# Chunk 3's decays repeated by DMA, convolution of z on VectorE, heads 0 and 1 made once, shares repeated in pieces

## The reference

```
x = norm(x + mamba_mixer_and_mlp(x))     # stage 0
x = norm(x + latent_attention_and_moe(x))# stage 1: 16 heads of 8, 7 routed experts, top 2
x = norm(x + linear_attention(x))        # stage 2: 4 heads of 64
x = norm(x + binary_mlp(x))              # stage 3
x = norm(x + attention(x))               # stage 4: 16 heads, score width 128
x = norm(x + moe(x))                     # stage 5: 8 experts of 256, top 2, gelu
x = norm(x + pruned_attention(x))        # stage 6: 16 heads of 64, keys masked by head 0's scores
x = norm(x + moe(x))                     # stage 7: 8 experts of 176, top 2, plus shared ones
```

```
xs, zs = split(in_proj(ln(x)));  xc, zc = silu(conv4(xs) + bx), silu(conv4(zs) + bz)
delta  = softplus(dt(xc));  dA = exp(delta * A);  dBu = delta * B * u
h_t    = dA_t * h_{t-1} + dBu_t;  y_t = sum over states of h_t * C_t
out    = out_proj(concat(y + u * D, zc))
S  = relu(masked scores of head 0);  FF = cumulative sum of shifted S;  att = att - FF
keep the 51 keys with the smallest FF and the diagonal, per query, for all heads
```

## Time and profile before

| | before |
|---|---|
| median of the runs | 1339.64 us |
| the profiled execution: time, span | 1339.95 us, 1338.2 us |
| TensorE busy | 1285.8 us, 96% |
| TensorE weight loads | 910.6 us, 68% |
| VectorE busy | 922.5 us, 69% |
| ScalarE busy | 909.0 us, 68% |
| GpSimd busy | 768.9 us, 57% |
| mean granted TensorE clock | 0.978 |
| moved by DMA | 67.87 MB |
| chain that ended last | 82% TensorE, 6% ScalarE, 5% GpSimd, 5% VectorE |

### The profile page before, as it was taken

The page is one execution under the profiler, slowest core; times in us unless marked ns, Lnnn a source line. Parts: engine busy times, 40 slices in busy tenths (PEclk is TensorE's granted clock), DMA queues, the critical chain, the costliest instruction groups (busy, mean ns, idle before and its releaser), DMA issues.

```text
span 1338.2 us, 26178 instructions
## 1 busy us (share of the span) xinstructions
PE 1285.8 (96%) x8764; PEld 910.6 (68%) x8764; DVE 922.5 (69%) x3611; ACT 909.0 (68%) x2503; POOL 768.9 (57%) x845
## 2 busy tenths in 40 slices
PE   8999789999998999999999999999999999999997
PEld 4445356567754777678777777777788877876665
DVE  5777998868757677757566454797597678764244
ACT  6667899777585789675868565557577758755221
POOL 2878877568539477476665755447534525442525
PEclk9679999999998999999999999999999999999999
DMA  8744000110042000102000101201200021004230
GB/s 291 190 127 108 1 2 1 57 57 2 1 142 85 1 2 2 57 24 104 4 1 1 64 1 38 92 1 64 83 2 1 2 80 17 2 1 135 55 103 24
DMA packets 23109, 67.87 MB, mean 51 GB/s; under 512 B 2336, under 2 KB 9120, under 8 KB 20672
## 3 DMA queue, kind: packets, MB, share of 16 engines
q1 hardware_dynamic: 22976, 66.20, 15.6%
HBM read 62.85 MB, written 3.34 MB: 49 GB/s over the span
## 4 chain that ended last, share of the span: by engine, by line
PE 82%; ACT 6%; POOL 5%; DVE 5%; issue 1%; DMA 1%; SPq 0%; POOLq 0%; DVEq 0%; ACTq 0%
PE bank L1193 71%; PE bank L1197 11%; ACT arena L1651 3%; POOL arena L2461 1%; ACT L1651 1%; POOL arena L2465 1%; DVE arena L1912 1%; ACT bank L1651 1%; DVE stats L1926 1%; DVE stats L1915 1%; POOL arena L2524 1%; POOL stats L2452 0%; DVE arena L2091 0%; POOL arena L2474 0%; DVE stats L1929 0%
## 5 line engine op out<-in xcount | busy, mean ns | idle before, releaser
L1651 ACT ACTIVATE arena<-arena 128x256 f32<-128x256 f32 (+4 forms) x804 | 355.8, 446 | 50.1 <-POOL arena L2517 26.5
L1651 ACT ACTIVATE arena<-bank 128x512 f32<-128x512 f32 (+2 forms) x347 | 183.8, 560 | 204.4 <-PE bank L1193 135.1
L1193 PE MATMUL bank<-XT,W 128*128 128x512 f32 (+1 forms) x752 | 293.3, 525 | 0.0
L2474 POOL TENSOR_TENSOR arena<-arena 128x512 f32<-128x512 f32 (+1 forms) x108 | 170.6, 1595 | 153.4 <-DVE arena L1912 50.0
L1193 PEld LDWEIGHTS bank<-W,arena 128*128 128x128 f32 x1888 | 227.9, 192 | 39.2 <-issue 32.0
L1193 PE MATMUL bank<-W,arena 128*128 128x128 f32 x1888 | 238.2, 276 | 1.3 <-DVE arena L2173 0.8
L1193 PE MATMUL bank<-arena 128*32 128x256 f32 (+8 forms) x2912 | 225.5, 334 | 9.8 <-POOL arena L2484 2.7
L2523 POOL TENSOR_TENSOR arena<-arena 128x256 f32<-128x256 f32 x192 | 119.2, 621 | 189.2 <-DVE arena L2163 188.9
L1193 PEld LDWEIGHTS bank<-arena 128*32 128x32 f32 (+4 forms) x2912 | 152.8, 152 | 83.4 <-issue 48.2
L2524 POOL TENSOR_TENSOR arena<-arena 128x512 f32<-128x512 f32 x192 | 201.5, 1049 | 0.0
L1197 PE MATMUL bank<-CF,arena 128*128 128x128 f32 x1312 | 184.0, 277 | 12.0 <-POOL arena L2524 5.3
(11 more groups left out here) (143 smaller groups left out, 1670.2 us busy)
## 6 DMA issues: line engine op xcount, KB each, us to landing
arena<-rws SPq DMA_DIRECT2D x8, 2048.0 KB, 7.5
arena<-rep SPq DMA_DIRECT2D x62, 256.0 KB, 5.3
arena<-rws SPq DMA_DIRECT2D x4, 1792.0 KB, 6.4
W<-w SPq DMA_DIRECT2D x2, 2124.0 KB, 8.2
arena<-rws SPq DMA_DIRECT2D x8, 384.0 KB, 10.1
W<-w SPq DMA_DIRECT2D x1, 2692.0 KB, 9.5
XT<-wkq SPq DMA_DIRECT2D x4, 512.0 KB, 6.0
W<-w SPq DMA_DIRECT2D x1, 2005.0 KB, 15.7
```

The source lines that it names most:

```text
L1193: return e.matmul(o, lhsT, rhs, start=start, stop=stop, skip_group_check=True)
L1651: return e.activation(o, a, func, **kw)
L2474: e.tensor_tensor(h, h, w, ALU.mult).then_inc(has["gw"], 1)
```

## The change

**Decays of chunk 3.** `BY_DMA = (3,)`. For this chunk `0.da` goes. `0.wd` writes delta to DRAM (`repd`), 16 `0.rd` read it repeated into two tiles in SBUF in turn, `0.dd` takes the exponential there, and the scan reads decay and h from SBUF.

```diff
+                elif name == "0.wd":
+                    on.wait_ge(*emptied(u("b", "0.dt", c)))
+                    e.dma_start(repd[c], step0(c, 0)).then_inc(d_wd[c], 16)
+                elif name == "0.rd":
+                    g = group0(n)
+                    on.wait_ge(d_wd[c], 16)
+                    if n >= 2:
+                        on.wait_ge(*scanned(c, n - 2))
+                    e.dma_start(spread0(c, n), repd[c][8 * g:8 * g + 8, :].unsqueeze(0).to_broadcast([16, 8, 512])).then_inc(d_rd[c][n % 2], 16)
...
+                elif name == "0.dd":
+                    g, a = group0(n), spread0(c, n)
+                    on.wait_ge(a_mat, 4)
+                    on.wait_ge(d_rd[c][n % 2], 16 * (n // 2 + 1))
+                    act(later(a), later(a), ACT.Exp, scale=am[:, g:g + 1], bias=am[:, 16 + g:17 + g]).then_inc(has["dA"], 1)
...
+                    if c in BY_DMA:
+                        on.wait_ge(*after("dA", "0.dd", c, n))
+                        e.tensor_tensor_scan(h, spread0(c, n), h, 0.0, ALU.mult, ALU.add).then_inc(has["st"], 1)
...
+        def spread0(c, q):
+            return ar(c, 9784 + q % 2 * 512, 512)
+
+        def scanned(c, q):
+            return after("st", "0.st", c, q) if c in BY_DMA else emptied(decays0(c, q))
```

```diff
+                    if n:
+                        mm(ps[:, :], wt(0, "win")[:, 128:256], s0(c, 1)).then_inc(full[b.i], 1)
+                        continue
...
+                    own(ts(s0(c, 7), bank[b.i][:, :], wt(0, "tz")[:, 1:2], None, ALU.mult))
+                    for k in (0, 2, 3):
+                        lo, hi = max(0, 1 - k), 256 - max(0, k - 1)
+                        on.wait_ge(*own.last())
+                        ins = stt(o3[:, :, lo:hi], z3[:, :, lo + k - 1:hi + k - 1], wt(0, "tz")[:, k:k + 1], o3[:, :, lo:hi], ALU.mult, ALU.add)
```

```diff
+        def heads6(c, u, n, i):
+
+            return head0(c, n, 1) if (u, i) == (4, 0) else (k6 if n else q6)(c, u)[:, i * 256:(i + 1) * 256]
+
+        def fresh6(u):
+
+            return (1,) if u % 4 == 0 else (0, 1)
...
-                        for i in range(2):
+                        for i in fresh6(n):
                             ins = mm(ps[:, i * 256:(i + 1) * 256], wt(6, w)[:, (2 * m + i) * 128:(2 * m + i + 1) * 128], xt)
```

```diff
+        for k in range(5 if s == 7 else 4):
+            add("er", k, ("ew", 0))
...
+                    if n < 4:
+                        E = slice(2 * n, min(2 * n + 2, BLOCKS[s] - SHARED[s]))
+                        m = (E.stop - E.start) * 512
+                        e.dma_start(to[:, 1024 * n:1024 * n + m], w[E, :].rearrange("e t -> (e t)").unsqueeze(0).to_broadcast([128, m])
+                                    ).then_inc(d_er[c][n], 16)
```

More of the change, by code:

```diff
@@ L271, in stage_steps @@
             add("0.h", j, ("0.m", 0))
-        add("0.o", 0, *[("0.h", j) for j in range(4)])
+        add("0.x", 0, ("0.y", 0), ("0.b", 0, PREP))
+        add("0.o", 0, ("0.x", 0), *[("0.h", j) for j in range(4)])
         add("0.e", 0, ("0.o", 0))
@@ L311, in stage_steps @@
         add("4.vz")
-        add("4.v", 0, ("4.vz", 0))
-        add("4.r", 0, ("load", 0, PREP, 4))
+        add("4.v", 0, ("4.vz", 0), ("4.c", 0, PREP))
         for i in range(16):
             add("4.qk", i, ("load", 0, PREP, 4), *([("4.ex", last_reader(i - 5))] if i >= 5 else []))
-        attention(lambda u: [("4.r", 0)] + [("4.qk", u // 2 * 4 + k) for k in range(4)], lambda u: [("4.v", 0)])
+        attention(lambda u: [("4.v", 0)] + [("4.qk", u // 2 * 4 + k) for k in range(4)], lambda u: [("4.v", 0)])
         add("4.y", 0, *[("4.pv", u) for u in range(UNITS)])
@@ L711, in order_of_steps @@
             if tiled(x) != tiles:
-                more = 0.16 if t < free[g] + 0.1 else 0.09
+                more = (0.0 if tiles == "q" else 0.095) if t < free[g] + 0.1 else 0.09
             elif t > free[g] + 0.1:
@@ L786, with network @@
 ROOM = 10912
[L789 removed]
+def network(nc, x, ws, wkq, cf, cb, rep, repd, rws, gs, out):
     with ExitStack() as ctx:
@@ L1311, in _ @@
                     w2 = wt(0, "w2") if s == 0 else bw3[:, 512:1024]
-                    if s == 0:
-                        for j in range(4):
-                            mm(ps[:, j * 128:(j + 1) * 128], cst("one", 1), wt(0, "b2", 0, 1), j == 0, False)
                     for j in range(4):
@@ L1436, in _ @@
                     on.wait_ge(*after("rt_w", "1.rt" if s == 1 else f"{s}.r", c))
-                    w = s3(c, 0) if s == 5 else router(s, c)
-                    for j in range(4 if s == 5 else 1):
-                        ins = e.transpose(bank[b.i][:, j * 128:(j + 1) * 128], w[:, 32 * j:32 * j + 128], cst("ident"))
-                    ins.then_inc(full[b.i], 1)
+                    e.transpose(bank[b.i][:, 0:128], router(s, c), cst("ident")).then_inc(full[b.i], 1)
                 elif name in ("1.up", "7.up"):
@@ L1535, in _ @@
                 elif name == "4.v":
-                    b, ps = first(name, c)
-                    for j in range(4):
-                        ins = mm(ps[:, j * 128:(j + 1) * 128], cols_(4, c)[:, j * 128:(j + 1) * 128], wt(4, "wv"))
-                    ins.then_inc(full[b.i], 1)
-                elif name == "3.b":
+                    on.wait_ge(*after("rk", "4.c", PREP))
+                    for k, (b, ps) in enumerate((first(name, c), second(name, c))):
+                        for j in range(2):
+                            js = slice((2 * k + j) * 128, (2 * k + j + 1) * 128)
+                            ins = mm(ps[:, j * 144:(j + 1) * 144], cols_(4, c)[:, js], values4())
+                        ins.then_inc(full[b.i], 1)
+                elif name in ("0.b", "3.b"):
                     b, ps = first(name, c)
@@ L1564, in _ @@
                     ins.then_inc(full[b.i], 1)
-                elif name == "4.r":
-                    b, ps = first(name, c)
-                    for k in range(4):
-                        on.wait_ge(*emptied(u("b", "4.a", PREP, k)))
-                    for j in range(4):
-                        ins = mm(ps[:, j * 16:(j + 1) * 16], cols_(4, c)[:, j * 128:(j + 1) * 128], pre[:, 48:64])
-                    ins.then_inc(full[b.i], 1)
                 elif name == "4.qk":
@@ L1726, in _ @@
                     b = u("b", name, c, n)
-                    on.wait_ge(*filled(b))
-                    act(s0(c, 6 + n), bank[b.i][:, :], ACT.Silu, bias=wt(0, "czb" if n else "cxb")).then_inc(done[b.i], 1)
+                    if n:
+                        on.wait_ge(*emptied(b))
+                        act(s0(c, 7), s0(c, 7), ACT.Silu, bias=wt(0, "czb")).then_inc(has["zc"], 1)
+                    else:
+                        on.wait_ge(*filled(b))
+                        act(s0(c, 6), bank[b.i][:, :], ACT.Silu, bias=wt(0, "cxb")).then_inc(done[b.i], 1)
                 elif name == "0.bc":
```

228 lines of the change are left out of this document (133 added, 95 removed), and 537 rows, old and new, of tables (EMITS, OPENS, PARTS, TURNS).

## The result

The changed kernel took 1357.63 us (median of 4 runs, 1354.12 to 1361.34) against 1339.80 for the kernel before, beside it on the same chip: ratio 1.0121, 95% interval 1.0095 to 1.0148, slower by 13 to 20 us. The forecast was 1331, its range 1310 to 1348, with 0.60 on faster. Over all sets of runs the kernel before lay between 1337.0 and 1347.8 us. The execution profiled after took 1354.93 us, span 1352.8.

What follows compares the result with a forecast made beforehand. TensorE was taken as the bound where saturated, with four engines near a common limit from 100 to 200 us. Terms -15.5 - 4 + 11 = -8.5 us gave 1331 us, own range 1322 to 1336, full range 1310 to 1348.

Steps and rivals of the forecast that it cites:

- TensorE's work removed, without the bias of `0.o`: Heads 0 and 1 once 6.9 us, 4.r in 4.v 2.9, 5.wt transposes 1.3, 5.bb 0.4, all counted as gain.
- bias of `0.o` off TensorE, `0.x` on GpSimd: Four one-row matmuls per chunk go for one 0.b: 4.0 us gained; 0.x's 1.3 us per chunk covered by 0.m and 0.h.
- convolution of z on VectorE: TensorE loses 7.7 us over chunks 2, 0 and 1, VectorE gets 2.8 a chunk: -4 us, from -8 to +6.
- chunk 3 by DMA: Chunk 3's scan stretch 14.1 us longer, 3.1 filled by 4.qk steps and 4.b: +11 us net, from +5 to +20.
- Work taken off TensorE is worth its full length wherever the stretch is saturated.: Rule for pricing removed TensorE work: full length in saturated stretches, only a part in the first 250 us.
- all of the 15.5 us: Matmul time removed from TensorE, placed after 230 us at 93 to 100% busy and all counted; bounds 12 and 16.
- half of what TensorE loses: Convolution of z: -4 us, with VectorE's work free for chunk 2 and up to 5.7 us on the path for chunks 0 and 1.
- two buffers and a round of repeat, exponential and scan: Chunk 3: each two states need one round, landing 4.0 us plus exponential, scan and semaphores: 6.2 us (5.3 to 7.5).
- that was so before: Chunk 3's exponentials need ScalarE's table, which 1.up of chunk 1 changes; taken as unchanged from before, no cost given.
- rival 2: Chunk 3's DMA round trip between 0.rd and 0.st makes the kernel slower: landing 5.3 us, round 7.5, 1351 us; chance 0.23.
- 0.1 us: Chunk 3: each scan longer by this with both operands in SBUF, 1 us in seven rounds, left in the range.
- the 12 at which I had said that I would be wrong: Sign against the prediction: a gain under 12 us outside the stretch of chunk 3's scans.

Runs made afterwards that it cites:

- e10: Kernel before, old order, with heads 0 and 1 once, 4.r in 4.v, one 5.wt transpose, masks, er pieces; chunk 3, z, 0.o bias stay on TensorE: 1335.6 us.
- e7: All edits of the changed kernel, chunk 3 by DMA and z on VectorE included, in the step order of the kernel before: 1371.1 us, ratio 1.0233 to before.
- e11: e10 plus only the bias of 0.o made as in the change (0.b once, 0.x on GpSimd): 1344.6 us, ratio 1.0023 to before.
- e12: e10 plus only the convolution of z on VectorE, for all four chunks: 1345.1 us, ratio 1.0022 to before.
- e5: Changed kernel's edits in the old order, but chunk 3's steps repeated by TensorE and not by DMA; z on VectorE: 1355.0 us, ratio 1.0104 to before.
- e1: Changed kernel in its new order, with chunk 3's steps repeated by TensorE into PSUM again: 1353.3 us, ratio 1.0081 to before.
- e2: e1 with the convolution of z back on TensorE too, for all four chunks: 1356.3 us, ratio 1.0116 to before.
- e14: Changed kernel in its new order, with the bias of 0.o by four one-row matmuls again, no 0.x: 1359.3 us, ratio 1.0143 to before.
- e15: Edits of e10 in the changed kernel's new order (chunk 3, z and bias of 0.o by TensorE): 1355.1 us, ratio 1.0103 to before.
- e4: e3 with each chunk 3 repeat waiting for the exponential two states back instead of its scan: 1346.6 us, ratio 1.0051 to before.
- e9: Kernel before, leaving out the matmuls for heads 0 and 1 in 6.qk of units 0 and 4 (values wrong): 1338.2 us, ratio 0.9962.
- e13: e11 with 0.x moved in GpSimd's order to right before the eviction of 0.o: 1338.6 us, ratio 0.9971 to before.
- e3: Changed kernel, with ScalarE writing chunk 3's exponentials into PSUM so its scans have one PSUM operand: 1353.9 us, ratio 1.0090 to before.
- e8: Changed kernel, with GpSimd's multiplications beside chunk 3's scans cut to 8 of 512 columns (results left out): 1355.8 us, ratio 1.0100 to before.

## Why the prediction was wrong

**The sum, term by term.** Starting from e10, edits on the old order add up: 1335.6 + 9.0 (`0.x`) + 9.6 (z) + 16.1 (chunk 3) = 1370.3, and e7, which has them all, took 1371.1. The changed kernel, with the order written for them, took 1357.6.

| term | forecast | measured, old order |
|---|---|---|
| TensorE's work removed, without the bias of `0.o` | -11.5 | -5.4 (-7.5 to -3.1), e10 |
| bias of `0.o` off TensorE, `0.x` on GpSimd | -4.0 | +9.0, e11 |
| convolution of z on VectorE | -4 | +9.6, e12 |
| chunk 3 by DMA | +11 | +16.1, e7 - e5 |
| the order of all steps rewritten | no term | -13.5, changed - e7 |
| sum | -8.5 | +15.8 (by the ratio 1.0121: +16.2) |

The last row but one is what is left over, so the sum is bound to come out; only e7 above is a check on it. Undone one by one in the new order, the same edits are worth much less: chunk 3 by DMA +4.3 us (changed - e1), z -3.0 (e1 - e2), `0.x` -1.6 (changed - e14), none of them clear of noise. With all three undone (e15) the kernel is still 13.8 us above the one before by its ratio. So in the changed kernel itself no single edit holds the loss. It goes with the new order (and the bank numbers that follow from it), in which e1 to e4 are slow too.

**1. "Work taken off TensorE is worth its full length wherever the stretch is saturated."** This is the step that failed first. The earlier trace rows gave 100.00 busy of 100.00 us, and I took all. e10, which has this term alone, got 5.4 us (3.1 to 7.5) of 11.5; e9 got about 0.7 of its 6.9. Time in which TensorE is busy can cover a wait for another engine: where a 6.qk step's removed matmuls had stood over such a wait, it showed as 0.60 us of idle time for GpSimd, and `4.r` at 427.66 had stood over 1.8 us of one. Not all that is missing has been found this way. I had also put all of the 15.5 us after 230 us. Three of the four bias steps of `0.o` in it lie at 112, 127 and 206 us, where TensorE was 84 to 93% busy, so by my own rule only a part of their 3 us should have counted.

**2. `0.x` costed at nothing.** I named its cover (`0.m` and `0.h`) and asked who waits for it. I didn't ask what it waits for and what is queued behind it on GpSimd. In the old order that is 9.0 us, 6.0 of them by its place (e13). In the changed kernel's own order it costs nothing that could be measured (e14), but the 4.0 us forecast as its gain didn't come either.

**3. z: "half of what TensorE loses".** VectorE at 89% was in the earlier trace rows and I had +6 as the end of the range; the old order gives +9.6. I had them free for chunk 2 and in part on the path for chunks 0 and 1; e12 shows 0.9 us for chunk 2 and 3.0 between two scans for chunk 0. In the new order no difference could be measured (e1 against e2). The profile of the changed kernel was 6 us ahead of before from 240 to 335 us, about as forecast, and lost that again by 400.

**4. Chunk 3.** The stretch was forecast at 46.7 us and measured 53.6 by the same two marks (398.33 to 451.94). The mechanism, two buffers and a round of repeat, exponential and scan, is right (e4: early repeats take 6.6 us off). The sizes: landing 3.4 us and not 4.0, which should have made it shorter; scans 1.92 and not 1.21, 11 us in all, of which 5 to 7 reach the path (e3, e8; with short scans e8's stretch is 46.9 us by the same marks); one round of 10.6 us by the order on ScalarE and VectorE, of which the prediction said "that was so before". It wasn't: before, no round took over 5.3 us. Pairs came 7.0 us apart ((447.24 - 398.33) / 7), where 6.2 was forecast and 7.5 stood for rival 2. Rival 2 had the right place and sign, with 1351, and wrong reasons (landings of 5.3 us).

I had weighed the scan's new form by two adds, 0.800 and 0.685 us, and put "0.1 us" into the range. Those two rows don't bear on it: nothing says what GpSimd did beside them. The Trainium skill has the rule in full (SBUF — State Buffer, Who interferes with whom): a VectorE instruction with two SBUF inputs contends with a GpSimd instruction that reads SBUF, the ports that they share are an exclusive lock, and issue order decides which of them waits. By that rule a scan waits for the rest of a 1.26 or 2.34 us instruction, and the trace agrees: scans of 1.2 us with none beside them or one that started later, 1.8 to 2.3 where one of 512 columns had started first, up to 3.3 with one of 1024. I had cited only the short form of the rule, as a contention without a size.

**5. No term for the order.** The diff rewrites the rank of nearly every step. I counted the steps moved past chunk 3's last product and took the rest as standing still. With the edits of e10 the new order costs 19.5 us, with all of them it saves 13.5; its effect isn't a constant that adds to the others.

What would have shown it, as the prediction put it: idle time 85 us where 75 was forecast, most of it near 400 us; TensorE busy for 1267 us and not 1252, while 44 us more of the span ran at 1.2 GHz (that this is the reason is not shown); VectorE slightly longer between 100 and 200 us (90.1 for 88.7). The gain outside the stretch was 6.0 us, under the 12 at which I had said that I would be wrong.

**Open.** Why the new order loses 4 to 8 us at the entry of chunk 3 is read from gaps, not tested, and most of what the new order costs in e15 has no cause shown; how far my own placing of chunk 3's decays in e1, e2 and e15 adds to it isn't known. How much of the differences in the first 150 us is variation from one execution to the next isn't settled: e9 shows 6 us of it up to 440 us.

## What to carry to other kernels

Price an instruction that you add to an in-order engine by what it waits for and what is queued behind it, before its own length. Before you move an operand from PSUM to SBUF, look at what GpSimd does beside the instruction: two SBUF operands turned 1.2 us scans into 1.9. Take 100% busy as a bound of a gain, not as the gain, and where a diff rewrites the whole order, try the edits one by one in the old order: here the smallest set of them (e10) beat both kernels.

## What the runs showed of the hardware that was not expected

- A scan of 512 elements takes 1.22 us with both operands in SBUF if GpSimd's instructions beside it are 8 columns wide, 1.92 us in the mean (1.19 to 3.33) if they are full, and 1.22 with one operand in PSUM beside full ones (e8, changed, e3). GpSimd's own instruction is longer by it too: 5.57 us for two of 2.35.
- A 256 KB repeat with two in flight landed in 3.0 to 5.3 us, median 3.4, while those queued in larger numbers kept their median of 5.2. The Trainium skill's line for a transfer from GpSimd's queue (DMA: Bandwidth & Descriptors, Anatomy of one DMA) gives an estimate of 2.6 us; none of these, issued by SyncE, landed that fast.
- The same instructions took 6 us more in the first 440 us in one profile (e9) than in another (before). I don't know what decides it; the longer one had the lower granted clock.
